# Moving the output projection's items of an attention step behind the step's products with V

## The chip, the cores and the metric

The kernel runs on one core of one Trainium2 chip. The metric is the device time of one execution in microseconds (us). Four compute engines work side by side, each on its own instruction list and in order: TensorE (PE, matrix products into banks of PSUM), VectorE (DVE), ScalarE (ACT) and GpSimd (POOL). SyncE (SP) issues the DMAs. They wait for each other by semaphores only.

## The reference, cut to what matters

Four attention layers follow one another on x (2048 rows of 256). Layers 0, 2 and 3 are alike ("big" layers): 16 heads of 64, keys and values from a context of 1601 rows, a bias on a few key columns, softmax, output projection, plus x. Layer 1 has 16 heads of 16 and is built by other functions, which the change doesn't touch.

```python
q = hidden_states @ Wq
k = encoder_hidden_states @ Wk
v = encoder_hidden_states @ Wv
logits = jnp.einsum('bhqd,bhkd->bhqk', q, k) * scale
logits = logits + col_bias[None, None, :, :]
probs = jax.nn.softmax(logits, axis=-1)
out = jnp.einsum('bhqk,bhkd->bhqd', probs, v)
out = out.transpose(0, 2, 1, 3).reshape(B, HW, HEADS * HEAD_DIM)
out = out @ Wo + bo
out = out + residual
```

## The kernel before, in words

**A head.** The 1601 keys lie in 13 key tiles of 128 rows (the last has 65), the 2048 queries in 4 chunks of 512. For a pair of key tile and chunk, `scores` makes two products into one of three banks ST, and ScalarE takes the exponential of it into a slot of P (`exps`). P has 7 slots, each one key tile; tile t of a head takes the slot of the tile seven before it. `values` multiplies P with V into the banks OA and OB, 16 matmuls for two key tiles. The sum over the keys is kept in `acc`: VectorE adds tiles 1 and 2 (`add`, two halves each), GpSimd tiles 3 to 12 one after the other, and `sums` of the head before (8 matmuls) turns `acc` into denominators in step 1 of the next head. A slot of P is free once V's product and the addition of its tile are done (`wait_added`).

**Steps.** A head has 7 steps, g = 0 to 6. Step g consists of the units of the next two key tiles (8 units: a `scores`, then one or two `s_tile`s), and then `values` for its own two key tiles, for which ScalarE is done by then. `s_tile` makes a product of keys and queries of the NEXT head into one of three banks SS, and VectorE takes its row maximum (`s_max`), since the row maximum enters the scores. So 64 such products and 64 maxima are spread over the steps of a head. In the last head of a layer (head 15) there is no next head in the layer: its units hold scores alone, and VectorE has no maxima; there VectorE adds tiles 5 to 10 too, and GpSimd tiles 3 and 4 only (`dve_tiles`, `pool_tiles`).

**The ring of SS.** The three banks are used in turn by four kinds of products, in the order that `ring_order` writes down: "s" (a key product), "m" (a transposed row of maxima), "o" (an item of the output projection) and "z" (a denominator). A product waits until the one three places before it in this order has been taken out of its bank (`wait_ring`): by VectorE, or for "z" by ScalarE. `DVE_AT` numbers VectorE's takings in the same order.

**The output projection.** Heads go in pairs. When a pair is done, its output On (128 rows: two heads of 64) is split in a high and a low part. ScalarE writes the high part (`output_hi`, chunks 0 and 1 in step 5 of the even head after the pair, chunks 2 and 3 at the end of step 1 of the next odd head, in the same two buffers, so they wait for the items that read the first two). GpSimd writes the low part (`output_lo`): chunks 0 and 1 in the even head ahead of its last key tile, chunks 2 and 3 at the start of the odd head. PE then has 8 items (2 column tiles x 4 chunks) of 3 matmuls (`output`, lines 1036 to 1038). In the odd heads 3, 5, ..., 15 they stand in steps 1 and 2, four in each, one at every second unit, between a `scores` and its `s_tile`s. VectorE adds each to x (`add_output`, line 1611, or 1608 for a layer's first pair) at the same place among its maxima.

**VectorE's order in a step.** First everything of the units, then the step's `add` (tile 1 in step 0, line 1581; tile 2 in step 1, line 1587), then, in step 2, `reciprocals` of the head before's denominators (line 1596). SP spreads these over the partitions by 8 DMAs (`spread`), and GpSimd's `divide` (line 838), one ahead of each of the key tiles 7 to 10, waits for that. In head 15 the `add` of step 2 is that of tile 5, which waits for GpSimd's addition of tile 4:

```python
                    else:
                        for t in PV[g]:
                            if t in dve_tiles(h):
                                add(H, t)
                    if h > 0 and g == 2:
                        reciprocals(H - 1)
```

Lines in the rows: PE 989 and 990 scores, 970 key product, 1000 values, 1009 sums, 1036 to 1038 output item, 1047 the last pair's output; DVE 1560 maximum; ACT 1321 exponential, 1228 a copy; POOL 870 addition of a key tile, 844 low part, 838 divide.

Of the kernel before, what the change touches and what calls it, by code (L numbers as in the profile page):

```python
# [18 lines left out]
PAIRS = HEADS // 2  # L19
QT, KT = NQ // P128, -(-NK // P128)  # L20
# [66 lines left out]
    return part(SUNITS, q - S_FROM, S_TO - S_FROM) if S_FROM <= q < S_TO else range(0)  # L87


def o_item(h, g, u):  # L90

    if h % 2 == 1 and h >= 3 and 1 <= g < 3 and u % 2 == 0:
        return 4 * (g - 1) + u // 2
    return None


def pair_ended(l, h):


    return l * PAIRS + (h - 2) // 2 if h % 2 == 0 and h >= 2 else None  # L100


def pair_going_out(l, h):

    return l * PAIRS + (h - 3) // 2 if h % 2 == 1 and h >= 3 else None
# [6 lines left out]
def takes_sums(h, g):  # L112
    return g == 1 and h > 0
# [32 lines left out]
def ring_order():  # L146

    out = []
    for l in range(BIG):
        first = l * HEADS  # L150
        for q in range(QITEMS):
            out += [("s", first, i) for i in q_tiles(q)]
            if q == ROW_ITEM:
                out.append(("m", first, 0))
        for h in range(HEADS):
            for g in range(STEPS):
                for u in range(len(units(h, g))):
                    if takes_row(h, g, u):
                        out.append(("m", first + h + 1, 0))
                    if o_item(h, g, u) is not None:  # L160
                        out.append(("o", l * PAIRS + (h - 3) // 2, o_item(h, g, u)))
                    ahead, tiles = s_tiles(h, g, u)
                    out += [("s", first + h + ahead, i) for i in tiles]
                if takes_sums(h, g):
                    out.append(("z", first + h - 1, 0))
        out += [("z", first + HEADS - 1, c) for c in range(2)]
        out += [("o", l * PAIRS + PAIRS - 1, i) for i in range(8)]
    return out
# [50 lines left out]
def attention_layers(nc, a):  # L219
    with ExitStack() as ctx:  # L220
# [12 lines left out]
        o = base  # L233
# [67 lines left out]
        o = main  # L301
# [513 lines left out]
        def _(gp):  # L815
# [30 lines left out]
            def head(H):  # L846
                first, l, h = adds_before(pool_tiles, H), H // HEADS, H % HEADS
                if pair_going_out(l, h) is not None:
                    for j in range(2, JQ):
                        output_lo(pair_going_out(l, h), j)  # L850
                for t in range(3, KT):
                    if t == KT - 1 and pair_ended(l, h) is not None:
                        for j in range(2):
                            output_lo(pair_ended(l, h), j)
                    k = rows_of(t)
                    if H % HEADS > 0 and t in (7, 8, 9, 10):
                        gp.wait_ge(pool_a, first + 2 * min(t - 3, len(pool_tiles(H % HEADS))))
                        divide(H - 1, t - 7)
                        gp.wait_ge(pool_on, 4 * H - 3 + t - 7)
                    if t not in pool_tiles(H % HEADS):  # L860
                        continue
                    for c in range(2):
                        q = slice(2 * c, 2 * c + 2)
                        out = acc[H % 2][0:k, q, :]
                        gp.wait_ge(act_p, HU * H + JQ * t + 2 * c + 2)
                        if t == 3:
                            gp.wait_ge(dve_a, added_by(dve_tiles, H, 2) - 1 + c)
                        else:
                            gp.wait_ge(pool_a, first + 2 * (t - 4) + c + 1)
                        gp.tensor_tensor(out, out, P[0:k, slot(H, t), q, :], ALU.add).then_inc(pool_a, 1)  # L870
# [22 lines left out]
            for l in range(BIG):  # L893
                for n in range(QITEMS * l, QITEMS * (l + 1)):
                    i = n % QITEMS % NSTG
# [11 lines left out]
        def _(pe):  # L907
            pe.wait_ge(pool_set, 4)
            pe.wait_ge(d_xin, 32)
            for i in range(QT // 2):  # L910
                at = BEFORE_AT["x", i, 0]
                wait_bank(pe, at)
                for k in range(4):
                    t, ct = 2 * i + k // 2, k % 2
# [78 lines left out]
            def values(H, t):  # L993
                k, e, n = rows_of(t), H % 2, H // 2
                if t == 0:
                    pe.wait_ge(d_v[n % 2], 16 * (n // 2 + 1))
                    wait(pe, act_o, 2 * H)
                for j in range(JQ):
                    r = 64 * (j % 2)
                    last = pe.matmul(OAB[j // 2][r:r + 64, :], Vp[n % 2][0:k, t, 64 * e:64 * e + 64],  # L1000
                                     P[0:k, slot(H, t), j, :], start=t == 0, stop=t == KT - 1)
                last.then_inc(pe_pv, 1)
# [25 lines left out]
            def output(n, i):  # L1028
                at, ct, j = RING_AT["o", n, i], i % CT, i // CT
                w, q = slice(ct * 128, (ct + 1) * 128), slice(j * 512, (j + 1) * 512)  # L1030
                if i == 0:
                    pe.wait_ge(dve_wol, split_before(n) + 1)
                if ct == 0:
                    pe.wait_ge(pool_onl, 4 * split_before(n) + j + 1)
                wait_ring(pe, at)
                pe.matmul(SS[at % 3][:, :], woh[:, w], Onh[:, j % 2, :], start=True, stop=False)
                pe.matmul(SS[at % 3][:, :], woh[:, w], Onl[:, q], start=False, stop=False)
                pe.matmul(SS[at % 3][:, :], wol[:, w], Onh[:, j % 2, :], start=False, stop=True).then_inc(pe_o, 1)
# [40 lines left out]
            def head(l, h):  # L1079
                H = l * HEADS + h  # L1080
                for g in range(STEPS):
                    for u, (on, t, j) in enumerate(units(h, g)):
                        scores(H + on, t, j)
                        if takes_row(h, g, u):
                            transpose_max(H + 1)
                        if o_item(h, g, u) is not None:
                            output(pair_going_out(l, h), o_item(h, g, u))
                        ahead, tiles = s_tiles(h, g, u)
                        for i in tiles:
                            s_tile(H + ahead, i)  # L1090
                    pe.wait_ge(act_p, HU * H + JQ * (PV[g][-1] + 1))
                    for t in PV[g]:
                        values(H, t)
                    if h + 1 == HEADS and g + 1 == STEPS:
                        last_sums(H)
                    if takes_sums(h, g):
                        sums(H - 1)
# [363 lines left out]
        def _(dve):  # L1461
# [81 lines left out]
            for qd in range(QUADS):  # L1543
                if qd < BIG:
                    key_rows(qd)
                for i in range(4):
                    m, u, n = 2 + 4 * qd + i, 4 * qd + 4 + i, 4 * qd + i
# [45 lines left out]
            def reciprocals(H):  # L1593
                dve.wait_ge(act_z, z_banks(H) + 1)
                wait(dve, d_r, r_spread(H - 1))
                dve.reciprocal(R4[:, :], Zs[:, :]).then_inc(dve_r, 1)
# [6 lines left out]
            def add_output(n, i):  # L1603
                dve.wait_ge(pe_o, 8 * n + i + 1)
                x, bank = xacc[:, i % CT, i // CT * 512:i // CT * 512 + 512], SS[RING_AT["o", n, i] % 3]
                if n % PAIRS == 0:
                    dve.wait_ge(d_small, 16 * (BIG + 1))
                    dve.scalar_tensor_tensor(x, bank[:, :], bo[:, n // PAIRS, i % CT:i % CT + 1], x, ALU.add, ALU.add)\
                        .then_inc(dve_ss, 1)
                else:  # L1610
                    dve.tensor_tensor(x, bank[:, :], x, ALU.add).then_inc(dve_ss, 1)  # L1611
# [12 lines left out]
            def head(l, h):  # L1624
                H = l * HEADS + h
                for g in range(STEPS):
                    for u in range(len(units(h, g))):
                        if takes_row(h, g, u):
                            max_row(H + 1)
                        if o_item(h, g, u) is not None:  # L1630
                            add_output(pair_going_out(l, h), o_item(h, g, u))
                        ahead, tiles = s_tiles(h, g, u)
                        for i in tiles:
                            s_max(H + ahead, i)
                    if g == ROW_STEP - 1 and h + 1 < HEADS:
                        head_max(H + 1)
                    if h + 1 < HEADS:
                        for t in dve_tiles(h)[g:g + 1]:
# [4 lines that stand above are left out]
                                add(H, t)  # L1643
                    if h > 0 and g == 2:
                        reciprocals(H - 1)
                    if g == 4 and pair_ended(l, h) is not None:
                        weights_lo(pair_ended(l, h))

# [174 lines left out]
```

## Time and profile before

| what | value |
|---|---|
| median of 3 runs | 4599.04 us (4597.13 to 4606.99) |
| profiled execution | 4599.72 us, span 4597.9 us |
| PE busy | 4495.0 us (98%), 20657 matmuls |
| DVE busy | 3081.4 us (67%) |
| ACT busy | 2309.8 us (50%) |
| POOL busy | 2827.0 us (61%) |
| scores, L989 and L990 | 1024.2 + 990.1 us, x2496 each |
| key products, L970 | 977.6 us, x3072 |
| values, L1000 | 658.3 + 641.3 us |
| exponentials, L1321 | mean 597 ns, x2496 |

Busy time is the time in which an engine worked on an instruction. The three big layers take about 1000 us each (their heads from 580, 2445 and 3550 us on); the small layer lies between the first and the second. The granted clock of PE is 0.987 of full speed over the span.

### The profile page before, as it was taken

To read this page: it belongs to the slowest core of one execution; us is meant where nothing else is said; L and a number is where in the kernel's file an instruction comes from. 1 tells how busy PE (TensorE), PEld (TensorE's weight loads), DVE (VectorE), ACT (ScalarE), POOL (GpSimd) and SP (SyncE) were. 2 spreads that over 40 slices of the span, in tenths; PEclk is the share of its full clock that TensorE was granted. 3 is DMA by queue.
4 is the path that set the end of the run, shared out by engine and by line. 5 is a ranking of instruction groups with operands and counts; after the bars stand their busy time and mean duration, and the time that the engine had idled before them with its cause. 6 is when DMAs were issued, how large, how long until landed. Compare 5 with 4: busy or idle time off the path is not lost.

```text
span 4597.9 us, 56871 instructions
## 1 busy us (share of the span) xinstructions
PE 4495.0 (98%) x20657; PEld 2841.8 (62%) x20657; DVE 3081.4 (67%) x5037; ACT 2309.8 (50%) x4121; POOL 2827.0 (61%) x1365
## 2 busy tenths in 40 slices
PE   8999999999999979999999999999999999999999
PEld 7888866666656545555556666666656656665664
DVE  3321467777777678777846777777767677777776
ACT  3222455554555436666655555555555545554553
POOL 0000368898889711111036988898884888898886
PEclk9999999999999979999999999999999999999999
DMA  4555832221222021011234222222216212222220
GB/s 151 180 187 166 283 86 63 68 69 45 67 64 52 13 39 16 12 15 16 57 97 123 67 59 53 64 69 49 56 45 223 63 37 67 64 69 53 59 48 29
DMA packets 124633, 349.68 MB, mean 76 GB/s; under 512 B 28085, under 2 KB 46005, under 8 KB 113338
## 3 DMA queue, kind: packets, MB, share of 16 engines
q1 hardware_dynamic: 124352, 346.04, 28.4%
q8 instruction: 163, 2.67, 0.2%
q14 instruction: 118, 0.97, 0.1%
HBM read 191.31 MB, written 120.31 MB: 68 GB/s over the span
## 4 chain that ended last, share of the span: by engine, by line
PE 92%; DVE 6%; issue 1%; DMA 1%; ACT 0%; SPq 0%; POOL 0%; DVEq 0%; ACTq 0%
PE ST L989 13%; PE SS L970 12%; PE ST L990 12%; PE OA L1000 12%; PE OB L1000 11%; PE ST L1134 5%; PE OA L1142 4%; PE SS L1120 3%; DVE acc L1581 3%; PE OB L1120 1%; PE SS L1009 1%; DVE mpart L1560 1%; PE ST L1065 1%; PE ST L1066 1%; PE ST L1067 1%
## 5 line engine op out<-in xcount | busy, mean ns | idle before, releaser
L870 POOL TENSOR_TENSOR acc<-acc,P 128x1024 f32<-128x1024 f32 x912 | 2216.6, 2460 | 299.5 <-DVE acc L1587 286.3
L1321 ACT ACTIVATE P<-ST 128x512 f32<-128x512 f32 (+1 forms) x2496 | 1463.7, 597 | 1260.8 <-PE ST L990 1117.5
L1560 DVE TENSOR_REDUCE mpart<-SS 128x1 f32<-128x400 f32 (+1 forms) x3072 | 1629.7, 570 | 669.7 <-PE SS L970 594.4
L989 PE MATMUL ST<-QX,KX 128*128 128x512 f32 (+1 forms) x2496 | 1024.2, 410 | 3.5 <-DMA QS<-mrow 1.7
L970 PE MATMUL SS<-KS,QS 68*128 68x400 f32 (+1 forms) x3072 | 977.6, 352 | 14.7 <-DMA QS<-stq 8.3
L990 PE MATMUL ST<-QS,KS 69*128 69x512 f32 (+1 forms) x2496 | 990.1, 397 | 0.0
L970 PEld LDWEIGHTS SS<-KS,QS 68*128 68x128 f32 x3072 | 583.9, 190 | 191.3 <-DVE xacc L1611 23.9
L989 PEld LDWEIGHTS ST<-QX,KX 128*128 128x128 f32 (+1 forms) x2496 | 463.9, 186 | 360.2 <-issue 272.8
L1000 PE MATMUL OA<-P,Vp 128*64 128x512 f32 (+1 forms) x2496 | 658.3, 606 | 0.0
L1000 PE MATMUL OB<-P,Vp 128*64 128x512 f32 (+1 forms) x2496 | 641.3, 592 | 0.0
L1420 ACT ACTIVATE PG<-ST 128x512 f32<-128x512 f32 (+1 forms) x832 | 426.3, 618 | 213.3 <-PE ST L1134 213.1
L879 POOL TENSOR_TENSOR On<-Oraw,Z 32x512 f32<-32x512 f32 x64 | 81.7, 1277 | 661.3 <-ACT Z L1228 657.7
L990 PEld LDWEIGHTS ST<-QS,KS 69*128 69x128 f32 (+1 forms) x2496 | 465.1, 186 | 10.3
L1666 DVE TENSOR_REDUCE mpart<-SS 128x1 f32<-128x400 f32 (+1 forms) x768 | 396.8, 564 | 83.6 <-PE SS L1120 83.5
L897 POOL TENSOR_TENSOR stq<-stw,stq 128x512 fp32r<-128x512 f32 x96 | 123.1, 1289 | 522.0 <-ACT stw L1228 520.3
L1000 PEld LDWEIGHTS OB<-P,Vp 128*64 128x64 f32 (+1 forms) x2496 | 179.1, 137 | 356.6 <-issue 356.6
L838 POOL TENSOR_TENSOR On<-Oraw,R 64x512 f32<-64x512 f32 x192 | 253.3, 1320 | 98.8 <-issue 44.8
L1000 PEld LDWEIGHTS OA<-P,Vp 128*64 128x64 f32 (+1 forms) x2496 | 149.3, 136 | 265.9 <-issue 179.1
L1581 DVE TENSOR_TENSOR acc<-P 128x1024 f32<-128x1024 f32 x96 | 209.9, 2225 | 25.7 <-ACT P L1321 25.7
L844 POOL TENSOR_TENSOR Onl<-On,Onh 128x512 fp32r<-128x512 f32 x84 | 140.8, 1694 | 120.6 <-ACT Onh L1228 120.6
L1142 PE MATMUL OA<-PG,Vg 128*32 128x512 f32 (+1 forms) x1664 | 201.5, 599 | 0.0
L1587 DVE TENSOR_TENSOR acc<-acc,P 128x1024 f32<-128x1024 f32 x132 | 194.8, 1523 | 1.1 <-ACT P L1321 0.8
(250 smaller groups left out, 4492.3 us busy)
## 6 DMA issues: line engine op xcount, KB each, us to landing
q_parts<-stq SPq DMA_DIRECT2D x96, 512.0 KB, 5.2
QX<-q_parts SPq DMA_DIRECT2D x96, 512.0 KB, 11.2
KX<-k_parts SPq DMA_DIRECT2D x48, 801.0 KB, 9.1
QS<-q_parts SPq DMA_DIRECT2D x45, 512.0 KB
R<-R SPq DMA_DIRECT2D x360, 64.0 KB, 2.0
v_tiles<-sv SPq DMA_DIRECT2D x24, 832.0 KB, 6.5
Vp<-v_tiles SPq DMA_DIRECT2D x24, 832.0 KB, 7.1
k_parts<-skh SPq DMA_DIRECT2D x48, 400.5 KB, 4.9
```

Of the source, the lines that this page charges most:

```text
L838: gp.tensor_tensor(On[64 * e:64 * e + 64, j * 512:(j + 1) * 512], Oraw[r, c, :], R[r, c, :], ALU.mult)\
L870: gp.tensor_tensor(out, out, P[0:k, slot(H, t), q, :], ALU.add).then_inc(pool_a, 1)
L970: pe.matmul(SS[at % 3][:, 0:w], QS[H % 3][0:SROWS, qt * 128:(qt + 1) * 128], KS[H % 3][0:SROWS, o:o + w], start=True, stop=True).then_inc( ...
L989: pe.matmul(bank, KX[H % 2][:, t * 128:t * 128 + k], QX[H % 2][:, q], start=True, stop=False)
L990: pe.matmul(bank, KS[H % 3][0:MXROW + 1, t * 128:t * 128 + k], QS[H % 3][0:MXROW + 1, q], start=False, stop=True).then_inc(pe_st, 1)
L1000: last = pe.matmul(OAB[j // 2][r:r + 64, :], Vp[n % 2][0:k, t, 64 * e:64 * e + 64], P[0:k, slot(H, t), j, :], start=t == 0, stop=t == KT - 1)
L1142: last = pe.matmul(OA[j * QD:j * QD + QD, :], Vg[0:k, t, g * QD:g * QD + QD], PG[slot(h, t) * JQ + j][0:k, :], start=t == 0, stop=t == KT - 1)
L1321: act.activation(P[0:k, slot(H, t), j, :], ST[n % 3][0:k, :], ACT.Exp, scale=SCALE).then_inc(act_p, 1)
L1420: act.activation(PG[slot(h, t) * JQ + j][0:k, :], ST[n % 3][0:k, :], ACT.Exp, scale=SCALE1).then_inc(gact_p, 1)
L1560: dve.tensor_reduce(mpart[H % 2][:, i // len(KCH), c:c + 1], SS[RING_AT["s", H, i] % 3][:, 0:w], AX.X, ALU.max).then_inc(dve_ss, 1)
L1581: dve.tensor_tensor(out, P[:, slot(H, 0), q, :], P[:, slot(H, 1), q, :], ALU.add).then_inc(dve_a, 1)
L1666: dve.tensor_reduce(mpart[h % 2][:, i // len(KCH), c:c + 1], GS[GRING_AT["s", h, i] % 4][:, 0:w], AX.X, ALU.max).then_inc(gdve_ss, 1)
```

## The change

The eight items of a pair leave the units. The four of a step now stand behind the step's `values`, ahead of `sums` (which are in step 1). VectorE's additions for them stand last in the step: behind `add`, and in step 2 behind `reciprocals` too. GpSimd makes the low parts of chunks 0 and 1 ahead of key tile 11 instead of ahead of key tile 12. The ring's order follows. No instruction is added or removed.

```diff
-def o_item(h, g, u):
-
-    if h % 2 == 1 and h >= 3 and 1 <= g < 3 and u % 2 == 0:
-        return 4 * (g - 1) + u // 2
-    return None
+def o_items(h, g):
+
+
+    return range(4 * g - 4, 4 * g) if h % 2 == 1 and h >= 3 and 1 <= g < 3 else range(0)
@@ ring_order
-                    if o_item(h, g, u) is not None:
-                        out.append(("o", l * PAIRS + (h - 3) // 2, o_item(h, g, u)))
                     ahead, tiles = s_tiles(h, g, u)
                     out += [("s", first + h + ahead, i) for i in tiles]
+                out += [("o", l * PAIRS + (h - 3) // 2, i) for i in o_items(h, g)]
                 if takes_sums(h, g):
                     out.append(("z", first + h - 1, 0))
@@ gpsimd head
-                    if t == KT - 1 and pair_ended(l, h) is not None:
+                    if t == KT - 2 and pair_ended(l, h) is not None:
                         for j in range(2):
                             output_lo(pair_ended(l, h), j)
@@ tensor head
-                        if o_item(h, g, u) is not None:
-                            output(pair_going_out(l, h), o_item(h, g, u))
                         ahead, tiles = s_tiles(h, g, u)
                         for i in tiles:
                             s_tile(H + ahead, i)
                     pe.wait_ge(act_p, HU * H + JQ * (PV[g][-1] + 1))
                     for t in PV[g]:
                         values(H, t)
+                    for i in o_items(h, g):
+                        output(pair_going_out(l, h), i)
@@ vector head
-                        if o_item(h, g, u) is not None:
-                            add_output(pair_going_out(l, h), o_item(h, g, u))
                         ahead, tiles = s_tiles(h, g, u)
                         for i in tiles:
                             s_max(H + ahead, i)
...
                     if h > 0 and g == 2:
                         reciprocals(H - 1)
+                    for i in o_items(h, g):
+                        add_output(pair_going_out(l, h), i)
```

## Rows read from the trace of the kernel before

**Rows 1.** The page's chain of waits, shares by engine.
```profile
PE 92%; DVE 6%; issue 1%; DMA 1%; ACT 0%; SPq 0%; POOL 0%; DVEq 0%; ACTq 0%
```

**Rows 2.** Windows (from:to, length, busy by engine, clock): head 8, step 1, units; values.
```profile
1106.23:1111.99 5.76, 5.76 (x28) 4.80 (x26) 5.61 (x11) 4.19 (x8) 0.00 (x0) 1.00 0.01 1
1111.99:1115.58 3.59, 3.59 (x17) 1.06 (x17) 2.95 (x4) 0.53 (x1) 1.63 (x1) 1.00 0.00 0
```

**Rows 3.** Windows: units with output items, odd heads; layer 0's head 3 first.
```profile
776.36:785.66 9.30, 9.11 (x40) 6.93 (x38) 8.46 (x14) 4.25 (x8) 3.96 (x2) 1.00 0.00 0
...
1168.18:1177.47 9.29, 9.06 (x41) 6.95 (x39) 8.40 (x14) 4.26 (x8) 4.09 (x2) 1.00 0.00 0
1182.05:1191.06 9.01, 9.01 (x42) 6.98 (x38) 6.57 (x13) 5.06 (x9) 9.01 (x5) 1.00 0.01 2
4398.21:4407.39 9.18, 9.06 (x41) 6.94 (x39) 8.29 (x14) 4.26 (x8) 3.97 (x2) 1.00 0.00 0
4411.97:4420.99 9.02, 9.02 (x43) 6.99 (x39) 6.57 (x13) 5.06 (x9) 9.02 (x5) 1.00 0.00 0
```

**Rows 4.** Timeline of PE (start, us, what [idle before <-releaser]): head 9, step 1.
```profile
1170.68 0.45 PE L970 MATMUL SS<-KS,QS 68*128 68x400 f32 x1 [0.23 <-DVE xacc L1611]
```

**Rows 5.** Chain of waits in order of time (start, us): head 9, end of step 1.
```profile
1177.54 1.01 PE OA L1000 x4
1178.55 0.86 PE OB L1000 x4
...
1182.12 0.43 PE ST L989
1182.55 0.23 PE ST L990
```

**Rows 6.** Timeline of DVE: tile 1's addition in heads 8, 9, 12; head 9's first output addition.
```profile
1103.24 4.14 DVE L1581 TENSOR_TENSOR acc<-P 128x1024 f32<-128x1024 f32 x2
...
1165.20 4.82 DVE L1581 TENSOR_TENSOR acc<-P 128x1024 f32<-128x1024 f32 x2
1169.94 0.68 DVE L1611 TENSOR_TENSOR xacc<-SS,xacc 128x512 f32<-128x512 f32 x1
...
1364.44 5.09 DVE L1581 TENSOR_TENSOR acc<-P 128x1024 f32<-128x1024 f32 x2
```

**Rows 7.** Windows: head 12, step 1, units.
```profile
1367.42:1373.88 6.46, 6.04 (x28) 4.73 (x26) 6.38 (x10) 4.21 (x8) 1.02 (x1) 1.00 0.00 0
```

**Rows 8.** Timeline of POOL: head 11, its first divide.
```profile
1333.60 1.26 POOL L838 TENSOR_TENSOR On<-Oraw,R 64x512 f32<-64x512 f32 x1 [1.44 <-issue]
```

**Rows 9.** Windows: head 15, steps 1 and 2, three layers; units without items; slow clock.
```profile
3421.29:3444.34 23.05, 21.93 (x98) 12.63 (x96) 11.82 (x11) 10.67 (x19) 20.63 (x11) 1.00 0.00 1
1556.76:1582.10 25.34, 23.39 (x99) 13.75 (x97) 11.77 (x11) 10.81 (x19) 21.40 (x11) 0.93 0.00 1
4525.16:4548.06 22.90, 21.86 (x99) 12.62 (x97) 11.73 (x11) 10.67 (x19) 20.57 (x11) 1.00 0.00 1
3444.34:3448.50 4.16, 4.16 (x19) 2.56 (x17) 4.16 (x3) 3.31 (x7) 0.00 (x0) 1.00 0.01 2
1560.90:1564.30 3.40, 3.40 (x9) 2.64 (x8) 0.90 (x2) 1.74 (x3) 3.40 (x2) 0.50 0.02 5
```

**Rows 10.** Timeline of PE: layer 2's head 15, its first item.
```profile
3423.14 0.47 PE L1036 MATMUL SS<-Onh,woh 128*128 128x512 f32 x1 [1.12 <-issue]
```

**Rows 11.** Timeline of POOL: layer 2, end of head 14 and head 15.
```profile
3410.47 11.34 POOL L870 TENSOR_TENSOR acc<-acc,P 128x1024 f32<-128x1024 f32 x4
3421.78 2.50 POOL L844 TENSOR_TENSOR Onl<-On,Onh 128x512 fp32r<-128x512 f32 x2
...
3434.18 9.44 POOL L870 TENSOR_TENSOR acc<-acc,P 128x1024 f32<-128x1024 f32 x4
```

**Rows 12.** Timeline of DVE: layer 2's head 15, tile 5's addition and the reciprocals.
```profile
3441.41 4.43 DVE L1587 TENSOR_TENSOR acc<-acc,P 128x1024 f32<-128x1024 f32 x2 [0.32 <-POOL acc L870]
3445.76 3.34 DVE L1596 RECIPROCAL R<-Zs 128x512 f32<-128x512 f32 x1
```

## The prediction, made before the changed kernel was run

> **What bounds the kernel.** I read the chain of waits first: 92% of it is PE, 6% DVE [rows 1]. PE streams, and what is left to gain are the small holes between its products. So the question is where PE's steps are longer than their matmuls, and I went to windows, one per step. In an even head's step 1 the units take 5.76 us and the values 3.59 [rows 2]. The four items of a step are 12 matmuls of 0.23 us [rows 5], 2.8 us, so a step with items should take 5.76 + 2.8 = 8.57. It takes 9.18 to 9.30 in step 1 and 9.01 to 9.02 in step 2 (the ranges over the 18 heads 3 to 13 of three layers are 9.10 to 9.31, with one of 10.29, and 8.97 to 9.14) [rows 3]. That is 1.06 us a head (18.20 - 17.14). Its cause is the ring of three SS banks: PE's key product waits for DVE's output addition [rows 4], because DVE begins step 1 late, from tile 1's addition, and an item puts one more taking between two maxima.
>
> **The heads 3 to 13, steps 1 and 2.** The items leave the units, so units come down to 5.76 plus what DVE's lateness still costs. This can be read from heads without items. In head 8 tile 1's addition ends at 1107.38, 1.15 us into the step, and the step is 5.76. In head 12 it ends at 1369.53, 2.11 into the step, and the step is 6.46 [rows 2, 6, 7]. So every us beyond 2.11 - 0.70 = 1.41 is lost. In head 9 it ends 1.84 into the step [rows 6], in most odd heads 1.74; 0.35 us stay. In step 1 the items now stand between two products of the other kind (values and sums), so PE changes kind twice more: the first group of values costs 1.01 against 0.86, the first score 0.43 against 0.23 [rows 5], 0.35 together. In step 2 it changes no more often than before. What is hidden: the four output additions of DVE (0.68 each [rows 6]) begin behind `add` or `reciprocals`, which lie beside the 3.59 us of values; item 3 needs only item 0's bank, and an item takes 0.7 us, as an addition does. Cost nothing, as long as DVE is done with its 3.34 us of reciprocals [rows 12] when item 4 ends (values 3.59 + 0.9 against 0.9 + 3.34: just so). Gain: 1.06 - 0.35 - 0.35 = 0.36 a head, 18 heads: -6.5 us. Bounds: 0 (the lateness grows by 0.36) and -19.1 (no loss stays).
>
> **Denominators sooner.** In step 2 the reciprocals no longer follow four items; they begin some 3.5 us sooner, and so does SP's spreading (its wait for the items comes behind it in SP's queue, and the next thing there is the row of maxima in step 5; that is hidden). In head 11 GpSimd waited 1.44 us for the spread R at its first divide [rows 8], ended later, ran beside DVE's tile 1 addition of head 12 (5.09 against 4.14 in head 8 [rows 6]), and the step lost 0.70 [rows 7]. There are five such steps after heads 3 to 13, with 0.70, 0.51, 1.00, 0.51 and 1.16: -3.9 us if all go. Bounds 0 and -3.9.
>
> **GpSimd later in odd heads.** Chunk 3's high part waits for item 3, which now ends behind the values; by my sum GpSimd starts tile 3 at 14.9 us into step 1 against 14.7, and PE is 0.4 ahead by the head's end. So its last addition overlaps DVE's tile 1 addition of the even head by some 0.6 us more. End of that: 1.15 becomes 1.45 to 1.75, cost 0.05 to 0.35 in 18 heads. I take 0.15: +2.7 us; bounds 0 and +7.
> The Trainium skill (SBUF — State Buffer, "SBUF: two separate sides") says that an instruction of VectorE with two SBUF inputs and one of GpSimd take a shared port pair exclusively, the other one standing still for a whole instruction. By that rule the overlap costs DVE all of it, 1.75 and 0.35 a head, +6.3 instead of +2.7 us. The trace rather shows both engines slowed: four GpSimd additions take 11.34 us beside two of DVE and 9.44 alone [rows 11], 1.9 us for both of DVE's.
>
> **Head 15, the last of each layer.** Here the order on DVE bites. In step 2 DVE now has, in this order: tile 5's addition, which waits for GpSimd's tile 4; the reciprocals; the additions of items 4 to 7. Item 7 needs the bank of item 4. Times from the start T of step 1. Units 4.16 [rows 9], values 3.59: 7.75. Items 0 to 3 with the change of kind: item 1 done at 9.5, item 3 at 10.9 (each 0.7, 0.2 for a semaphore; estimate from the neighbouring starts). ScalarE's copies take about 0.6, GpSimd's low parts 1.25 each [rows 11]: chunk 3 ready at 12.9. GpSimd's four halves of tiles 3 and 4, 9.44 [rows 11]: 22.3, the same as before (3434.18 is T + 12.9). DVE's addition of tile 5 ends 2.2 us behind GpSimd (3445.84 against 3443.62 [rows 11, 12]): 24.5. Reciprocals 3.34 [rows 12]: 27.9. Item 4's addition 0.68: 28.6. Item 7: 29.4, where step 3 starts. PE has come to item 7 at 7.75 + 4.2 (items, sums of 1.0) + 4.16 + 3.59 + 2.3 = 22.0: it stands 6.6 us. Before, step 3 started at T + 23.05, 25.34 and 22.90 [rows 9]. Loss 6.35 + 4.06 + 6.50 = 16.9 us. The 25.34 holds a hole and the slow clock behind it, and all three hold a wait of 1.0 to 2.0 us for the first low part [rows 10], which the change does take away; that is in the sum.
> Two costs on top. First, the low parts sooner: GpSimd's tile 11 of head 14 ends 2.5 us later [rows 11], at T + 3.0 instead of T + 0.5, and tile 5's exponentials of head 15 need its slot at about T + 2.8. DVE's tile 2 addition, no longer behind items, now runs beside it and slows it by up to 1.9: T + 4.9. So PE is held 0.1 to 2.1 us, one more in layer 0, where tile 11 ended 0.8 later. I take 1.3, 1.3 and 2.0: +4.6; bounds 0 and +7. In the other heads tile 11 ends before step 1 starts, so the move is free. Second, the clock. After a hole of 1.95 us in layer 0 PE ran 3.40 us at half speed, 1.2 GHz, granted 0.50 [rows 9], which costs 1.7 us; after 1.12 us it did not fall (its window in [rows 9] has 1.00 throughout) [rows 10]. After 6.6 us I expect it each time: +5.1; bounds 0 and +15 (three times as long a stretch).
> Nothing later swallows this: DVE's ten additions of tiles 6 to 10 shift by some 2.6 us, PE by 6 to 8, and PE came to the last sums 2.3 to 3.4 us behind DVE already.
>
> **The sum.** -6.5 - 3.9 + 2.7 + 16.9 + 4.6 + 5.1 = +18.9 us on the profiled execution's 4599.72 (span 4597.9 and 1.8 around it), 4618.6. The median is 0.7 lower: 4618.
>
> **Rivals.**
> A, the gain in full and head 15 as computed without its extras: all 1.06 us go in 18 heads (DVE has no items to take while it catches up) and the five late steps: -19.1 - 3.9 + 16.9 = -6.1, 4593. With the extras in part, -6 to +6. For it: rows 3 in step 2 lose 0.45 with no late addition ahead. Against it: head 12's step without items loses 0.70. Within 0.2%: chance 0.13.
> B, the other side: faster. One mechanism: item 4's addition gets to DVE before PE comes to item 7, at T + 22.0. It needs GpSimd's tile 4 by T + 16, 6 us sooner than by the rows, since tile 3 must wait for chunk 3's low part. Then the three stretches of rows 9, 71.3 us in all, come down to 3 x 22.3 (two steps of 4.16 + 2.8 + 3.59, and 1.2 for the sums), -4.4 us, and the rest gives -7.7 to -23: 4571 to 4587. Chance 0.06.
> C, head 15 worse: the clock stays low for 10 us behind each hole and the even heads lose 0.35 each: 4618 + 10 + 3.6 = 4632. Chance 0.08.
> D, that the items don't leave the critical stretch at all in heads 3 to 13 (same loss before and behind): +6.5 on my sum, 4625; it counts with the forecast.
>
> **Chances.** Forecast with D 0.73, A 0.13, C 0.08, B 0.06. 0.2%, what a measurement of this kernel can tell from no change, is 9.2 us: slower means above 4608.2, faster below 4589.8. Slower: 0.73 and 0.08 less a little for small sizes, 0.79. Same 0.14, faster 0.07. The range reaches from A's upper end to C: 4600 to 4630.
>
> **What would show it.** In head 15's step 2, item 7 (line 1036) after a hole of 5 to 8 us in each big layer, released by DVE line 1611, and the granted clock at 0.50 behind it; step 3 starting 29 to 32 us after step 1. In odd heads, units of 5.8 to 6.3 us and an extra change of kind in step 1. POOL line 838 without idle time in heads 3 to 13. Wrong if item 7 follows item 6 at once, or if odd heads save more than 1 us each.

## The result and the profile after

| | before | after |
|---|---|---|
| median of 6 runs | 4602.91 us | 4622.26 us (4618.27 to 4627.20) |
| profiled span | 4597.9 us | 4620.8 us |

The ratio is 1.0045, with a 95% interval of 1.0035 to 1.0056: slower, by 19.4 us in the medians and 22.9 us in the two traces. The page of the changed kernel, its chain of waits by engine (answers to [rows 1]):

```profile
PE 91%; DVE 4%; POOL 2%; issue 2%; DMA 1%; SPq 0%; ACT 0%; POOLq 0%; DVEq 0%; ACTq 0%
```

GpSimd, which had no share, has 2% now: somewhere the end hangs on it. To find where, I laid the starts of all steps of both traces side by side. In heads 0 to 14 the changed kernel is faster in each big layer, by 3.6, 4.3 and 4.6 us (12.5 together). In head 15 it loses 10.3, 13.7 and 10.4 us (34.4 together); the rest of the span makes +1.0.

**Head 15.** The holes of PE there, layers 0 and 2 (timeline of PE, after; the first pair is layer 0's, the second layer 2's, and layer 3 has 1.93 and 6.49):

```profile
1557.36 0.79 PE L987 MATMUL ST<-QX,KX 128*128 128x512 f32 x1 [2.97 <-ACT P L1319]
1583.75 0.80 PE L1034 MATMUL SS<-Onh,woh 128*128 128x512 f32 x1 [6.50 <-DVE xacc L1609]
...
3428.33 0.79 PE L987 MATMUL ST<-QX,KX 128*128 128x512 f32 x1 [2.01 <-ACT P L1319]
3456.20 0.79 PE L1034 MATMUL SS<-Onh,woh 128*128 128x512 f32 x1 [6.51 <-DVE xacc L1609]
```

The second of each pair is item 7. What VectorE does meanwhile in layer 2 (timeline of DVE, after; answers to [rows 12]):

```profile
3447.88 4.46 DVE L1585 TENSOR_TENSOR acc<-acc,P 128x1024 f32<-128x1024 f32 x2 [8.46 <-POOL acc L868]
3452.26 3.34 DVE L1594 RECIPROCAL R<-Zs 128x512 f32<-128x512 f32 x1
3455.52 1.82 DVE L1609 TENSOR_TENSOR xacc<-SS,xacc 128x512 f32<-128x512 f32 x3
3457.88 0.69 DVE L1609 TENSOR_TENSOR xacc<-SS,xacc 128x512 f32<-128x512 f32 x1 [0.55 <-PE SS L1036]
```

Read from below: item 7's product begins at 3456.20, as soon as item 4's addition (the first of the three at 3455.52) has freed the bank; that addition stands behind the reciprocals, those behind tile 5's addition, and that one idled 8.46 us for GpSimd. And GpSimd (timeline of POOL, after; answers to [rows 11]):

```profile
3417.46 4.48 POOL L842 TENSOR_TENSOR Onl<-On,Onh 128x512 fp32r<-128x512 f32 x2
3421.91 10.31 POOL L868 TENSOR_TENSOR acc<-acc,P 128x1024 f32<-128x1024 f32 x4
3438.11 2.66 POOL L842 TENSOR_TENSOR Onl<-On,Onh 128x512 fp32r<-128x512 f32 x2 [5.89 <-ACT Onh L1226]
3440.74 9.38 POOL L868 TENSOR_TENSOR acc<-acc,P 128x1024 f32<-128x1024 f32 x4
```

Its first two low parts took 4.48 us, where they took 2.50 before [rows 11]; VectorE's tile 2 addition (3418.51, 4.52 us) ran beside them. Tile 11, the first half of the next row's four, came late for it, and the hole of 2.01 us in step 1 is the wait for its slot. Windows of the same stretches (after; columns as in [rows 2]): PE runs at half speed behind both holes.

```profile
3422.61:3439.61 17.00, 14.99 (x54) 6.75 (x53) 3.17 (x5) 5.50 (x10) 11.02 (x6) 0.80 0.00 1
3439.61:3457.64 18.03, 11.52 (x48) 6.38 (x45) 9.46 (x6) 4.64 (x9) 10.50 (x5) 0.84 0.03 6
...
3428.33:3434.66 6.33, 6.33 (x15) 1.98 (x16) 0.00 (x0) 1.53 (x3) 3.89 (x2) 0.50 0.00 0
3456.20:3461.91 5.71, 5.71 (x13) 4.46 (x14) 5.16 (x7) 2.39 (x4) 0.00 (x0) 0.50 0.38 93
```

The first two are steps 1 and 2: 35.03 us, against 23.05 before [rows 9].

**Heads 3 to 13.** Windows of the units in steps 1 and 2 of layer 3's head 13 (after):

```profile
4409.45:4415.53 6.08, 6.07 (x28) 4.74 (x26) 6.01 (x10) 4.21 (x8) 3.96 (x2) 1.00 0.00 0
4423.06:4428.89 5.83, 5.83 (x31) 4.83 (x27) 4.53 (x9) 4.81 (x9) 5.83 (x3) 1.00 0.00 0
```

They answer to 9.18 and 9.02 with the items inside [rows 3]. Means over the 18 odd heads 3 to 13 of the three layers, from the start of one step to that of the next: step 1 13.82 before and 13.70 after, step 2 12.60 and 12.24, step 3 9.37 and 9.27.

### The profile page after: what moved, and what is told of

Same layout as the page of the kernel before. It is cut to its first block, busy times and chain, and to the rows that moved or that the text cites. A ratio compares the mean times of both kernels' runs of the same rounds, so it can differ in the third digit from the quotient of the medians.

```text
span 4620.8 us, 56871 instructions
## 1 busy us (share of the span) xinstructions
PE 4500.9 (97%) x20657; PEld 2845.0 (62%) x20657; DVE 3078.6 (67%) x5037; ACT 2311.0 (50%) x4121; POOL 2812.7 (61%) x1365
## 4 chain that ended last, share of the span: by engine, by line
PE 91%; DVE 4%; POOL 2%; issue 2%; DMA 1%; SPq 0%; ACT 0%; POOLq 0%; DVEq 0%; ACTq 0%
PE ST L987 13%; PE SS L968 12%; PE ST L988 12%; PE OA L998 12%; PE OB L998 11%; PE ST L1132 5%; PE OA L1140 4%; PE SS L1118 3%; DVE acc L1579 1%; POOL acc L868 1%; PE OB L1118 1%; PE SS L1034 1%; PE SS L1007 1%; PE ST L1063 1%; PE ST L1064 1%
## 5 line engine op out<-in xcount | busy, mean ns | idle before, releaser
L968 PE MATMUL SS<-KS,QS 68*128 68x400 f32 (+1 forms) x3072 | 967.7, 350 | 10.6 <-DMA QS<-stq 8.2
L842 POOL TENSOR_TENSOR Onl<-On,Onh 128x512 fp32r<-128x512 f32 x84 | 112.8, 1353 | 161.8 <-ACT Onh L1226 160.4
L1585 DVE TENSOR_TENSOR acc<-acc,P 128x1024 f32<-128x1024 f32 x132 | 181.2, 1421 | 25.4 <-POOL acc L868 25.4
```

What stands on the lines that cost most here:

```text
L968: pe.matmul(SS[at % 3][:, 0:w], QS[H % 3][0:SROWS, qt * 128:(qt + 1) * 128], KS[H % 3][0:SROWS, o:o + w], start=True, stop=True).then_inc( ...
```

## The experiments

All edits are against the changed kernel unless the text says otherwise; the ratios are to the kernel before, timed in the same group of runs. The groups are E1 to E4 (before: 4599.42), then E5, E6 and E8 (before: 4598.29), then E9 to E11 (before: 4600.11). The kernel before moves by up to 5 us from one group to another, so medians of different groups are compared by their ratios. Step lengths are read from the traces.

**E1, head 15's additions for the items first.**

```diff
+                    if h + 1 == HEADS:
+                        for i in o_items(h, g):
+                            add_output(pair_going_out(l, h), i)
                     if g == ROW_STEP - 1 and h + 1 < HEADS:
...
-                    for i in o_items(h, g):
-                        add_output(pair_going_out(l, h), i)
+                    if h + 1 < HEADS:
+                        for i in o_items(h, g):
+                            add_output(pair_going_out(l, h), i)
```

> The changed kernel, with one difference: in head 15 alone VectorE's additions for the items stand ahead of its addition of a key tile and of the reciprocals. Theory (item 7 of head 15 waits for item 4's addition, which is queued behind tile 5's addition and the reciprocals): the three holes of 6.5 us ahead of item 7 go, and the slow clock behind them (step 3 is 8.8 to 9.5 us against 7.7), together 24 us: 4598, ratio to the kernel before 0.999 (0.998 to 1.000). The holes of 2 to 3 us in step 1 of head 15 stay. Rival (the items cost that time wherever they stand in head 15, since GpSimd's tiles 3 and 4 come late and PE only waits elsewhere): the hole moves to a later score or to the last sums, and the time stays above 4612.

Measured: 4588.82 us, ratio 0.9973 (0.9963 to 0.9983). No hole ahead of item 7 is left; step 2 of head 15 is 10.6 us in each layer, where it was 18.03. The theory's side, but 9 us better than expected, since the holes in step 1 shrank too, which I had not expected: VectorE's tile 2 addition is late again, behind the items. The only one left (timeline of PE, E1):

```profile
1559.34 0.50 PE L987 MATMUL ST<-QX,KX 128*128 128x512 f32 x1 [0.74 <-ACT P L1319]
```

**E2, E1 with the low parts of chunks 0 and 1 ahead of tile 12 again.**

```diff
-                    if t == KT - 2 and pair_ended(l, h) is not None:
+                    if t == KT - 1 and pair_ended(l, h) is not None:
```

> As the run before, and GpSimd's low parts of chunks 0 and 1 stand ahead of key tile 12 again, as before the change. Theory: head 15 keeps none of its losses; the holes in step 1 (2.97, 2.01 and 1.93 us, and the slow clock behind them) go too, 11 us more than the run before: 4587, ratio 0.9965 (0.995 to 0.998). What is left is the gain of heads 3 to 13, some 12 us by the two traces, and 6 us of head 15's first holes. Rival (the slot of key tile 11 is late because VectorE's tile 2 addition now runs beside GpSimd, not because of the low parts): the holes in step 1 stay at 1 us or more, 4594.

Measured: 4583.96 us, ratio 0.9967 (0.9954 to 0.9980). Step 1 of head 15 is 11.70, 11.69 and 11.71 us (16.48, 17.00 and 13.84 in the changed kernel), with no hole. In heads 0 to 14 it is as the changed kernel. The theory holds, but little was left for it: of the 11 us expected on top of E1, E1's steps 1 had already saved 10.8, and E2's are 1.4 us shorter still. The medians are 4.9 us apart; the rest of that no row shows, and the two intervals overlap.

**E4, the changed kernel with E2's line alone.**

> The changed kernel, with the low parts of chunks 0 and 1 ahead of key tile 12 again. Theory: the holes of 2 to 3 us in step 1 of head 15 and the slow clock behind them go (11 us), those of 6.5 us ahead of item 7 stay: 4611, ratio 1.002 (1.001 to 1.003). Rival (VectorE's tile 2 addition beside GpSimd is what makes the slot late): half of it stays, 4617.

Measured: 4611.03 us, ratio 1.0025 (1.0015 to 1.0035), as the theory has it. The holes of 6.5 us stay, those of step 1 fall from 2.97, 2.01 and 1.93 us to 0.52, 0 and 0 (timeline of PE, E4, the first holes and layer 2's item 7):

```profile
1555.18 0.50 PE L987 MATMUL ST<-QX,KX 128*128 128x512 f32 x1 [0.52 <-ACT P L1319]
...
3450.00 0.79 PE L1034 MATMUL SS<-Onh,woh 128*128 128x512 f32 x1 [6.52 <-DVE xacc L1609]
```

E1, E4 and the changed kernel together show that the wait for tile 11's slot needs both causes: sooner low parts alone give 0.74 us in three layers, the sooner tile 2 addition alone 0.52, both 6.91.

**E3, the kernel before with the sooner low parts alone.** The line of E2 the other way round, on the kernel before.

> The kernel before, with the low parts of chunks 0 and 1 ahead of key tile 11: the third part of the change alone. Theory: in head 15 the wait for the first low part (1.0 to 2.0 us ahead of item 0) goes, and tile 5's exponentials wait for their slot for 0 to 1 us instead: -5 us in all, 4598, ratio 0.999 (0.998 to 1.0005). Nothing in heads 3 to 13. Rival (the sooner low parts hold PE by themselves, as in the changed kernel): holes of 2 us or more in step 1 of head 15 and a time 3 to 7 us above the kernel before.

Measured: 4592.80 us, ratio 0.9989 (0.9980 to 0.9999), interval just below 1. Steps 1 of head 15 are 11.32, 11.34 and 11.29 us against 15.03, 12.69 and 12.61: the wait for the first low part is gone, and no slot is waited for. That is 6.4 us in head 15, as the theory has it. (The profiled execution took 4602.43 us, the longest of the ten. It has 6.7 us more in step 1 of heads 12 and 13 of layer 2: in head 12 a hole of 1.04 us, 0.71 in the kernel before, with a granted clock of 0.69 over the step behind it, and in head 13 one of 1.80 us. Why they are longer here no run shows.)

**E8, head 15's reciprocals behind the items, tile 5's addition still ahead.**

```diff
-                    if h > 0 and g == 2:
+                    if h > 0 and g == 2 and h + 1 < HEADS:
                         reciprocals(H - 1)
                     for i in o_items(h, g):
                         add_output(pair_going_out(l, h), i)
+                    if g == 2 and h + 1 == HEADS:
+                        reciprocals(H - 1)
```

> The changed kernel, with one difference: in head 15's step 2 VectorE makes the items' additions ahead of the reciprocals, still behind tile 5's addition. Theory (the 6.5 us are tile 5's addition and 3.34 us of reciprocals in a row): each hole ahead of item 7 falls to 3.2 us (3.0 to 3.4), -10 us and at most 3 us of slow clock: 4611, ratio 1.002 (1.001 to 1.003). Rival (it is the wait for GpSimd's tile 4 alone, the reciprocals being hidden): the holes stay above 6 us.

Measured: 4609.59 us, ratio 1.0026 (1.0015 to 1.0037), 0.0019 or some 9 us below the changed kernel; in the traces head 15 is 11.1 us shorter. Item 7 of the three layers (timeline of PE, E8):

```profile
1579.74 0.50 PE L1034 MATMUL SS<-Onh,woh 128*128 128x512 f32 x1 [3.27 <-DVE xacc L1609]
...
3445.65 0.79 PE L1034 MATMUL SS<-Onh,woh 128*128 128x512 f32 x1 [3.30 <-DVE xacc L1609]
...
4552.60 0.50 PE L1034 MATMUL SS<-Onh,woh 128*128 128x512 f32 x1 [3.29 <-DVE xacc L1609]
```

So the 6.5 us are 3.2 of reciprocals and 3.3 of waiting for GpSimd's tile 4 and adding tile 5.

**E5, E2 with the items behind the sums.** In `ring_order` and in TensorE's head the "z" stands ahead of the "o"s of a step, and ScalarE takes the denominators ahead of chunks 2 and 3's high parts:

```diff
-                    if takes_sums(h, g - 1):
+                    if takes_sums(h, g - 1) and pair_going_out(l, h) is None:
                         take_z(H - 1)
...
                     if g == 1 and pair_going_out(l, h) is not None:
+                        take_z(H - 1)
```

> The second run's kernel (head 15's additions first, low parts of chunks 0 and 1 late), with step 1's order on PE turned: values, sums, items instead of values, items, sums, and ScalarE's copy of the denominators ahead of chunks 2 and 3's high parts in the odd heads with items. Theory (the items between two products of the other kind cost 0.35 us in each of 21 heads): -7 us, less 1 to 3 us where GpSimd starts 1 us later and runs longer beside VectorE's tile 1 addition of the even heads: 4579, ratio to the kernel before 0.9955 (0.994 to 0.997); step 1 of an odd head 13.3 us long instead of 13.6. Rival (no cost in the change of kind; GpSimd's lateness decides): step 1 stays at 13.6, even heads go from 10.5 to 10.9, 4590.

Measured: 4632.09 us, ratio 1.0065 (1.0051 to 1.0079). A miss, and worse than the rival too. Steps 1 and 2 of an odd head are 13.59 and 12.13 us (medians of 18), against 13.64 and 12.23 in E2: by this the change of kind (between fp32r products, the scores and items, and fp32 ones, the values and sums, which also have narrower tiles; no run separates the two) costs some 0.2 us, not 0.35. The even heads' step 1 goes from 10.5 to 11.7 in 14 of 18, to 14.9 in one and to 16.5 in three; two of the odd heads that follow such a slow one take 20 us. In layer 0's head 6 (timelines of POOL, DVE and PE, E5):

```profile
959.18 15.08 POOL L868 TENSOR_TENSOR acc<-acc,P 128x1024 f32<-128x1024 f32 x6
```

```profile
969.57 5.78 DVE L1580 TENSOR_TENSOR acc<-P 128x1024 f32<-128x1024 f32 x2
```

```profile
973.78 0.53 PE L968 MATMUL SS<-KS,QS 68*128 68x400 f32 x2
975.88 0.45 PE L968 MATMUL SS<-KS,QS 68*128 68x400 f32 x1 [1.11 <-DVE mpart L1559]
976.92 0.54 PE L968 MATMUL SS<-KS,QS 68*128 68x402 f32 x1
978.10 0.54 PE L968 MATMUL SS<-KS,QS 68*128 68x400 f32 x1
```

GpSimd works until 974.26, so VectorE's tile 1 addition, 2.35 us when it runs alone, takes 5.78; the maxima are late, PE has a hole of 1.11 us, and behind it the key products come 1.2 us apart instead of 0.65. The window from 976.28 to 981.50 has a granted clock of 0.50. All 18 even heads have this hole, of 1.04 to 1.13 us; the 14 of 11.7 us keep the full clock behind it.

**E9, E2 with VectorE making the low parts of chunks 2 and 3**, behind its additions for step 1's items; PE waits for them by a semaphore of their own.

```diff
-                    for j in range(2, JQ):
-                        output_lo(pair_going_out(l, h), j)       # gpsimd
...
+                        for j in range(2, JQ) if g == 1 and pair_going_out(l, h) is not None else ():
+                            output_lo(pair_going_out(l, h), j)   # vector, behind add_output
```

> The second run's kernel, with VectorE making the low parts of chunks 2 and 3 (behind its additions for the items of step 1) instead of GpSimd. Theory (even heads lose time in step 1 by how late GpSimd ends tile 12 beside VectorE's tile 1 addition): GpSimd starts tile 3 of an odd head some 4 us sooner, at the end of VectorE's tile 2 addition, the even heads' step 1 falls from 10.5 to 10.35, -3 us against the second run: 4581, ratio to the kernel before 0.996. The odd heads stay (13.65 and 12.25), since low part 3 ends 0.6 us into step 2 and maxima are late from 1.4 on. Rival (something else makes the even heads 10.5): no change there, and VectorE's 1.4 us of low parts cost PE 0.3 to 1 us in step 2.

Measured: 4692.13 us, ratio 1.0197 (1.0183 to 1.0211). The even heads' step 1 fell to 10.36 us (medians: 10.51 in E2, 10.48 in E11, the same kernel), as the theory of GpSimd's lateness has it; the 10.36 is what heads without any stall take. GpSimd's last addition now ends 6.0 us ahead of that step, and VectorE's tile 1 addition runs alone, in 2.35 us. But the odd heads before it are longer too, which also gives GpSimd time: in E6 below GpSimd keeps its low parts, ends 3.9 us ahead, and the step is 10.36 as well. So E9 shows that the cost goes when GpSimd is done in time, not what the low parts alone are worth. The time is missed by far: step 2 of the odd heads is 18.8 to 19.0 us in 15 of 18, 17.3 in one and 14.2 in two, instead of 12.2. VectorE's two low parts ran beside GpSimd's additions, which now started sooner (timelines of DVE, POOL and PE, E9, head 9):

```profile
1190.59 3.63 DVE L1604 TENSOR_TENSOR Onl<-On,Onh 128x512 fp32r<-128x512 f32 x2
1194.15 2.00 DVE L1558 TENSOR_REDUCE mpart<-SS 128x1 f32<-128x400 f32 x4
...
1185.30 20.43 POOL L865 TENSOR_TENSOR acc<-acc,P 128x1024 f32<-128x1024 f32 x8 [4.08 <-DVE acc L1585]
...
1194.77 0.70 PE L965 MATMUL SS<-KS,QS 68*128 68x400 f32 x1 [1.65 <-DVE mpart L1558]
```

I had put them at 1.4 us. The maxima start 3.3 us into the step, PE has a hole of 1.65 us, and then half the clock for the rest of the units (window of E9). The two heads of 14.2 us have the same hole, of 1.69 us, and the full clock behind it, so the slow clock is 4.8 us of the 6.7 lost:

```profile
1194.80:1202.00 7.20, 7.20 (x19) 5.73 (x21) 4.37 (x9) 2.95 (x5) 7.20 (x4) 0.50 0.01 2
```

**E10, E5 with the same move.**

> The kernel with the items behind the sums (values, sums, items), with VectorE making the low parts of chunks 2 and 3. Theory (that kernel's loss of 48 us against the second run is GpSimd's 1 us of lateness, over the edge where the maxima come late, PE gets a hole of 1 us and in some heads the slow clock behind it): the even heads' step 1 falls from 11.7 (and 16.5) to 10.4, the odd heads' step 2 grows from 12.1 to 12.5 to 13, as the low part of chunk 3 ends 2.1 us into it: 4586, ratio 0.997. Rival (the loss comes from the sums ahead of the items): even heads stay at 11.7, above 4620.

Measured: 4747.06 us, ratio 1.0315 (1.0301 to 1.0329). The even heads are back at 10.36 us from 11.7 with the sums still ahead of the items, so the sums' place costs them nothing by itself (GpSimd ends 6.0 us ahead of the step, again partly since the odd heads are longer). What E5's rows show is GpSimd's end: it comes 1.7 us into the step, VectorE's tile 1 addition takes 5.72 to 5.80 us, and the hole follows. The forecast of the time fell for the reason of E9, with step 2 of the odd heads at 20.3 to 22.4 us.

**E6, E2 with the items' additions first in every head.**

> The second run's kernel, with VectorE's additions for the items ahead of its key tile addition and of the reciprocals in every head, not in head 15 alone. Theory (the reciprocals' place decides when the denominators are spread; behind the items they are 6 us later than in the changed kernel, and GpSimd waits for them at its first divide, then runs beside the next tile 1 addition): POOL's divide waits 3 us in each head 3 to 13, the even heads' step 1 goes from 10.5 to 11.2 us or more, +13 us against the second run: 4597, ratio 0.9995. Rival (VectorE's place for the items doesn't matter in heads 3 to 13): 4584, the even heads stay at 10.5.

Measured: 4771.33 us, ratio 1.0374 (1.0360 to 1.0389). Both theory and rival were wrong. GpSimd's first divide waits 2.9 to 6.9 us, as much as the theory had or more, but the even heads stay at 10.36 us, since the odd heads grow by more than that. Their steps 2 and 3 go from 12.2 and 9.3 us to 14 to 17 and 15 to 17. With the items' products behind the values, additions that stand first push tile 2's addition and the reciprocals to the start of the next step's maxima (timelines of DVE and PE, E6, head 9, start of step 3):

```profile
1227.51 2.75 DVE L1609 TENSOR_TENSOR xacc<-SS,xacc 128x512 f32<-128x512 f32 x4 [5.81 <-PE SS L1036]
1230.18 3.34 DVE L1594 RECIPROCAL R<-Zs 128x512 f32<-128x512 f32 x1
1233.44 2.43 DVE L1558 TENSOR_REDUCE mpart<-SS 128x1 f32<-128x402 f32 x5
...
1234.01 0.45 PE L968 MATMUL SS<-KS,QS 68*128 68x400 f32 x1 [2.50 <-DVE mpart L1558]
```

PE's fourth key product of that step starts behind a hole of 2.50 us at 1234.01, and the slow clock follows (0.59 from there to 1240.50). So in these heads VectorE's additions are better last, as the change has them; in head 15, where no maxima follow, they are better first.

**E11, E2 once more.**

> The second run's kernel again (items behind values everywhere, head 15's additions for them ahead of key tile additions and reciprocals, low parts of chunks 0 and 1 ahead of tile 12), with more rounds: 4584 to 4587, ratio to the kernel before 0.9967 (0.996 to 0.9975), as a base for the two others of this set.

Measured: 4584.90 us, ratio 0.9965 (0.9953 to 0.9978), as before. By the ratios E2 beats both kernels: 15 to 16 us below the kernel before, 37 below the changed one.

## Why the prediction was right, point by point

- **The order on VectorE in head 15** was the decisive step, and it came out nearly to the number: holes of 6.50, 6.51 and 6.49 us against 6.6 forecast, each ahead of item 7. In layer 3, where the wait for the slot brought no slow clock, step 3 starts 31.87 us behind step 1; I had 29.4 plus 1.3 for the slot. E1 takes the holes away, E8 halves them.
- **The low parts sooner** did hold head 15 by tile 11's slot: 6.9 us of holes against 4.6 taken, in my bounds of 7. That it needs VectorE's tile 2 addition beside it is what E1 and E4 show.
- **The clock.** Of the 5.1 us about 6 came behind the holes at item 7 (4.2 in the three steps 3, 0.6 in each item 7). Not in my sum: it fell behind the slot's holes too, in layers 0 and 2, some 5 us (step 1 of layer 2 is 17.00 us, of layer 3 13.84, with holes of nearly one length). With the slot's 2.3 us this is the largest error: head 15 lost 34.4 us, 26.6 forecast.
- **Heads 3 to 13** gained 0.585 us each in steps 1 to 3 (35.79 to 35.21), 10.5 together, not 6.5. The term that was too large is the change of kind: E5 puts it at 0.2 us, and 18 x 0.15 is most of the difference. Rival A's gain in full (1.06 each) did not come: the units of step 1 take 6.10 us in the median against 5.76, so VectorE's lateness still costs the 0.35 forecast.
- **The denominators sooner:** as forecast. Even heads' steps 1 of 10.88 to 11.54 us, five of them before, are all at 10.46 to 10.51 after, and GpSimd's waits for the spread denominators ahead of its first divide in the five heads before them, 1.29 to 1.85 us, are gone (one of 1.0 us in layer 0's head 14 stays).
- **GpSimd later:** the other even heads went from 10.36 to 10.48, 0.12 against the 0.15 taken. In head 8 the addition of tile 1 (after)

```profile
1098.73 4.51 DVE L1579 TENSOR_TENSOR acc<-P 128x1024 f32<-128x1024 f32 x2
```

  ends 1.52 us into the step; the edge of 1.41 read from [rows 6, 7] gives 0.11. The edge holds elsewhere too: an end at 2.40 us cost 1.01 in the kernel before (layer 2's head 12), one at 1.71 cost 0.28 in the changed kernel (layer 3's head 6), and one at 2.79 cost 1.37 in E5. The Trainium skill's exclusive port (SBUF — State Buffer, "SBUF: two separate sides") had given 0.35. The number was too large, but the trace agrees with the rule, once the instructions are looked at one by one. Here are VectorE's two halves of tile 1 and GpSimd's last addition, in head 8 before and then after:

```profile
1102.78 2.38 POOL L870 TENSOR_TENSOR acc<-acc,P 65x1024 f32<-65x1024 f32 x1
1103.24 3.01 DVE L1581 TENSOR_TENSOR acc<-P 128x1024 f32<-128x1024 f32 x1
1106.17 1.21 DVE L1581 TENSOR_TENSOR acc<-P 128x1024 f32<-128x1024 f32 x1
...
1098.73 1.22 DVE L1579 TENSOR_TENSOR acc<-P 128x1024 f32<-128x1024 f32 x1
1098.80 3.36 POOL L868 TENSOR_TENSOR acc<-acc,P 65x1024 f32<-65x1024 f32 x1
1099.87 3.38 DVE L1579 TENSOR_TENSOR acc<-P 128x1024 f32<-128x1024 f32 x1
```

  Before, VectorE's first half came while GpSimd's addition ran, and ended 1.1 us, nearly its own length, behind it. After, it came 0.07 us ahead: GpSimd's addition took its usual 2.4 us and 1.0 more, and VectorE's second half ended 1.1 us behind GpSimd. So each waits for the other's whole instruction, in turn, and what looks like two slowed engines in the prediction's row (11.34 against 9.44) is this turn-taking: two of GpSimd's four additions took 1.0 us longer each. The estimate of 0.35 counted the growth of the overlap; what counts is which instruction comes first, and then the end of GpSimd's last one, plus 1.1 us. E9's 3.63 us for two subtractions shows the same.
- **The sum.** -12.5 + 34.4 + 1.0 = +22.9 us between the traces against +18.9: two errors of 5 and 8 us with opposite signs, so that the total came this near is partly luck. The medians differ by 19.4, for which 18.9 was forecast.

## What to carry to other kernels

When work is moved to the end of a step, check the step that is built differently from the others: here the last head of a layer, where the instruction ahead of the moved one waits for another engine, and a ring of three banks hands that wait to PE. Put moved work behind long instructions only where those neither wait themselves nor end later than the ring needs the moved work (by E8 half of the 6.5 us was the length of the reciprocals), and ahead of them only where nothing urgent follows. An edge can be read before the run from steps of the same trace that are late by different amounts; a plan that sits 0.1 us beyond it, as the even heads here, leaves no room for the next engine's microsecond.

## What the runs showed of the hardware

A short hole of PE can cost far more than itself. E5's 1.11 us hole was followed by 5 us at a granted clock of 0.50 and made the step 4.8 us longer than the even heads' steps that have the same hole and keep the clock (16.49 against 11.73); E9's 1.65 us was followed by 7.2 us. The length of a hole alone doesn't decide: the clock stayed full behind 1.12 us in the kernel before [rows 10] and 1.93 us in the changed one. Counted over heads 1 to 15 (to step 3) of the big layers in all twelve profiles, a granted clock of 0.50 came within 3 us behind none of 12 holes of 0.7 to 1.0 us, 5 of 26 of 1.0 to 1.2, 3 of 5 of 1.2 to 1.4, 30 of 37 of 1.4 to 1.8, 4 of 8 of 1.8 to 2.1, and all 47 longer ones. What decides among holes of one length was not settled. The Trainium skill (TensorE: Matmul & The Clock Gate, "A second HAM failure mode: psum-queue depth-cycling") says that frequent small idles of PE between groups of matmuls, as it cycles through PSUM banks, can make the clock swing between its two levels. Here too the holes of E5, E6 and E9 are waits for a bank, and the clock went between 1.00 and 0.50; but in these traces one such hole in a step was enough.

Where additions of VectorE and GpSimd in SBUF overlap in these traces, each waits for the other's whole instruction: two of VectorE's additions took 2.35 us alone and 5.78 beside GpSimd in E5, and GpSimd's two low parts 2.50 and 4.48.
